# Joining maxima by one reduction, low parts after the transpose, fewer waits: one change to a fused transformer kernel in seven places

## The chip, the core and the metric

One NeuronCore of a Trainium2 chip. The metric is the device time of one execution in microseconds: 2005.45 us, the median of three runs (2004.56 to 2005.53). Engines: PE (TensorE, matrix products, with its weight loads as PEld), DVE (VectorE), ACT (ScalarE), POOL (GpSimd), SP (SyncE, here only a queue of DMAs). Each has a queue of its own, worked off in order; they meet by semaphores only.

## The reference

Two transformer blocks one after the other, everything in float32, on x of 2 x 1024 x 256 and a context of 2 x 77 x 192, 16 heads each:

```
block 0: x += attention(ln(x), ln(x))        16 heads of 64
         x += attention(ln(x), context)      16 heads of 64
         x += (a * gelu(gate)) @ ff_w2       a, gate = split(ln(x) @ ff_w1 + b)
block 1: the same with heads of 16, biases on q, k and v, a causal mask in the
         self attention, gelu(ln(x) @ mlp1) @ mlp2 as the hidden layer
attention: softmax(q k^T / sqrt(d)) v @ w_out + b_out
```

## The kernel before

Stages run one after the other, each in a block that ends in a barrier of all engines: `constants`, `project_norm` (output product, residual sum, layer norm, transposed into `hT`; PE queue: `product(i)`, `turn(i - 1)`), `wide_attention` (self attention of block 0, 34 to 895 us), `cross_attention` wide, `hidden_layer`, `thin_attention`, `cross_attention` thin, `hidden_layer`.

**Wide self attention.** `both(g, b)` works on two heads (group g of 8) of batch b. It has 8 units `u` of two steps; a step is one key tile of 128 for one half `h` of 512 queries (16 steps: half 0, then half 1). In a step PE makes scores for two heads (`scores`: three products of rounded high and low parts, and a fourth that subtracts the row's maximum, from `m_rows`), ACT takes the exponential into one of four buffers `p_buf`, POOL adds them up into `acc` (`both` on POOL, L1235; step 0 and step 8 have no addition), and one unit later PE makes the weighted sums (`weighted`, L998). Between these, PE works ahead for the next batch or group: the `lanes` tables say which item belongs to which unit. Items are `("k", c)` and `("q", c)` (projection; ACT writes the high part, DVE the low part), `("v", c)`, `("m", qt, half)` (one 128 x 512 score tile for each of two heads, only for its maxima: two PE products L935, two DVE reductions L1142 into `mx`), `("t", h)` (L941: the transpose of the maxima of four query tiles, DVE's copy of it into `m_turned` L1150, and from there SP's DMAs into `m_rows` L864) and `("den", h)` (sum over the keys). All items use three PSUM banks in turn, in a fixed order: an item may be filled when DVE (or ACT) has emptied the one three places before. A unit has two `m` items, unit 7 has three, and the first pass (0, 0) has three in some more.

When DVE has reduced the last tile of four (`("m", 3, 1)` in unit 5, `("m", 7, 1)` in unit 1), it joins: `join` (L1157, L1160, L1162) takes the larger of two halves' maxima, its negative rounded, and what the rounding left, each with a wait on the one before. DVE also inverts the denominators (L1171, in quarters; units 2, 3, 6, 7), multiplies the outputs by them (`normalise`, L1177, units 0 and 4 of the next pass) and splits the weights of the next group (`split_w`, L1113, at the end of unit 6, for b = 0).

**Cross attentions.** 32 units n (pair of heads, 512 queries). PE's slot n is `score(n)` (four products L1386), `query(n + 1)` (L1373; in the thin one for every fourth n), `weighted(n - O_LAG)` (L1400), `turn(n - T_LAG)` (L1414), with O_LAG, T_LAG = 2, 1 (wide) and 3, 2 (thin). One PSUM bank `o_ps` holds the weighted sums; DVE's `copy(n - C_LAG)` (L1553 wide, L1556 thin; C_LAG 3 and 4) empties it and raises `o_done`. DVE's slot is `invert(n - 1)`, `copy(n - C_LAG)`, `take(n)` in the wide one and `copy`, `take`, `invert` in the thin one; `take` reads the scores (L1527 or L1519 first), `invert` sums the exponentials (L1541) and inverts (L1545). ACT's slot in the wide one is the copy of the turned probabilities (L1468), the copy of the queries (L1452), the exponential (L1460); thin: exponential, queries, turned. `lin(g, b, per, k)` is the count that a semaphore has after k events of pass (g, b).

## Time and profile before

| | us |
|---|---|
| median of three runs | 2005.45 |
| the profiled execution | 2007.0 |
| its span | 2005.3 |
| busy: PE / PEld / DVE / ACT / POOL | 1788.9 / 1121.9 / 1238.4 / 794.2 / 874.5 |
| L1142 DVE, maxima, x512 | 328.7, mean 0.685 |
| L935 PE, tiles of the maxima, x512 | 130.0, mean 0.502 |
| L1157, L1162 DVE, in the join, x32 each | 30.3 and 34.3, means 0.946 and 1.071 (medians 0.169) |
| L1113 DVE, split of weights, x8 | 0.693 / 2.074 / 2.589 (least, median, most) |
| L1235 POOL, additions, x224 | 532.4, means 2.379 and 2.364 |
| L1386 PE, cross attention scores, x512 | 78.2, mean 0.294 |
| mean granted clock of TensorE | 0.962 |

PE, DVE, ACT and POOL overlap, so their busy times don't add up; what counts in a stage is the engine that never waits and what its idle time waited for. The table's means and medians belong together: where they are far apart, some of the instructions were held. In the rows below, a line in order of time has the start, the duration, the engine, the line, the operation, what it writes and reads, how many were merged, and in brackets the idle time before it with what ended it.

### The profile page before, as it was taken

To read this page: it belongs to the slowest core of one execution; us is meant where nothing else is said; L and a number is where in the kernel's file an instruction comes from. 1 tells how busy PE (TensorE), PEld (TensorE's weight loads), DVE (VectorE), ACT (ScalarE), POOL (GpSimd) and SP (SyncE) were. 2 spreads that over 40 slices of the span, in tenths; PEclk is the share of its full clock that TensorE was granted. 3 is DMA by queue.
4 is the path that set the end of the run, shared out by engine and by line. 5 is a ranking of instruction groups with operands and counts; after the bars stand their busy time and mean duration, and the time that the engine had idled before them with its cause. 6 is when DMAs were issued, how large, how long until landed. Compare 5 with 4: busy or idle time off the path is not lost. (4 is left out here: it accounts for less than half of the span.)

```text
span 2005.3 us, 29769 instructions
## 1 busy us (share of the span) xinstructions
PE 1788.9 (89%) x10124; PEld 1121.9 (56%) x10124; DVE 1238.4 (62%) x2173; ACT 794.2 (40%) x1315; POOL 874.5 (44%) x767
## 2 busy tenths in 40 slices
PE   3789999999999999979899998997798986898799
PEld 2455555555555545538555587886444434565678
DVE  4667777777777777733566443345788853787600
ACT  3234444444444444431344313221366662344340
POOL 1356666666666666661122300021156664366110
PEclk9799999999999999989999898998699998999899
DMA  1000000000000000003000001003244421000101
GB/s 53 6 4 7 4 7 3 6 3 6 3 6 3 6 3 0 1 29 91 24 1 1 1 1 51 21 17 55 51 76 77 87 45 28 8 1 1 29 17 42
DMA packets 49440, 43.69 MB, mean 22 GB/s; under 512 B 17920, under 2 KB 44060, under 8 KB 49343
## 3 DMA queue, kind: packets, MB, share of 16 engines
q1 hardware_dynamic: 44991, 35.86, 8.0%
q0 software_dynamic: 4352, 6.56, 1.6%
q8 instruction: 58, 0.95, 0.2%
q14 instruction: 39, 0.32, 0.0%
HBM read 22.84 MB, written 2.24 MB: 13 GB/s over the span
## 5 line engine op out<-in xcount | busy, mean ns | idle before, releaser
L1235 POOL TENSOR_TENSOR x<-x,sa_p_buf 128x1024 f32<-128x1024 f32 x192 | 456.8, 2379 | 177.6 <-ACT sa_p_buf L1056 169.8
L1056 ACT ACTIVATE sa_p_buf<-sa_score 128x512 f32<-128x512 f32 x512 | 275.9, 597 | 350.8 <-PE sa_score L985 340.7
L1142 DVE TENSOR_REDUCE sa_mx<-sa_front 128x1 f32<-128x512 f32 x512 | 328.7, 685 | 120.4 <-PE sa_front L935 119.0
L998 PE MATMUL sa_out<-sa_p_buf,sa_v_buf 128*64 128x512 f32 x1024 | 246.1, 602 | 0.0
L1722 POOL TENSOR_TENSOR x<-x,bias_out 128x1024 f32<-128x1024 f32 x24 | 55.7, 2348 | 278.6 <-POOLq L1907 152.8
L528 ACT ACTIVATE sa_p_buf<-sa_score 128x1024 f32<-128x1024 f32 (+1 forms) x160 | 141.1, 938 | 86.3 <-PE sa_score L476 86.1
L342 DVE TENSOR_REDUCE sa_mx<-sa_front 128x1 f32<-128x512 f32 (+1 forms) x256 | 155.9, 650 | 26.1 <-PE sa_front L283 23.1
L935 PE MATMUL sa_front<-sa_k_hi,sa_q_hi 64*128 64x512 f32 x512 | 130.0, 502 | 43.3 <-DVE sa_mx L1142 41.2
L935 PEld LDWEIGHTS sa_front<-sa_k_hi,sa_q_hi 64*128 64x128 f32 x512 | 49.6, 186 | 185.1 <-DVE sa_mx L1142 79.4
L1235 POOL TENSOR_TENSOR x<-sa_p_buf 128x1024 f32<-128x1024 f32 x32 | 75.6, 2364 | 133.0 <-ACT sa_p_buf L1056 133.0
L1611 POOL TENSOR_TENSOR ca_probs<-ca_s_sb,ca_inv 128x616 f32<-128x616 f32 x64 | 77.9, 1218 | 125.7 <-DVE ca_inv L1545 125.7
L998 PEld LDWEIGHTS sa_out<-sa_p_buf,sa_v_buf 128*64 128x64 f32 x1024 | 65.0, 136 | 115.3 <-issue 85.8
L1171 DVE RECIPROCAL x<-x 128x128 f32<-128x128 f32 x128 | 111.9, 918 | 26.3 <-ACT x L1069 26.3
L283 PE MATMUL sa_front<-sa_k_top,sa_q_top 59*128 59x128 f32 (+4 forms) x576 | 87.1, 369 | 40.4 <-DVE sa_mx L342 29.5
L283 PEld LDWEIGHTS sa_front<-sa_k_top,sa_q_top 33*128 33x128 f32 (+1 forms) x576 | 53.5, 207 | 102.3 <-DVE sa_mx L342 82.8
L1740 PE MATMUL po_prod<-w_out,o 128*128 128x256 f32 x384 | 92.2, 400 | 20.7 <-PEq L415 11.6
L580 POOL TENSOR_SCALAR_AFFINE_SELECT sa_p_buf<-sa_p_buf 128x128 f32<-128x128 f32 x256 | 65.0, 292 | 96.5 <-ACT sa_p_buf L528 96.4
L981 PE MATMUL sa_score<-sa_q_hi,sa_k_hi 64*128 64x512 f32 x512 | 102.8, 394 | 0.0
L985 PE MATMUL sa_score<-sa_m_rows,sa_one_rows 64*128 64x512 f32 x512 | 102.1, 390 | 0.0
L981 PE MATMUL sa_score<-sa_q_lo,sa_k_hi 64*128 64x512 f32 x512 | 102.1, 391 | 0.0
L981 PE MATMUL sa_score<-sa_q_hi,sa_k_lo 64*128 64x512 f32 x512 | 102.0, 391 | 0.0
L1468 ACT ACTIVATE ca_turned<-ca_t_ps 128x1024 f32<-128x1024 f32 x64 | 65.5, 1023 | 78.2 <-PE ca_t_ps L1414 78.2
(189 smaller groups left out, 3378.4 us busy)
## 6 DMA issues: line engine op xcount, KB each, us to landing
x<-in_x SPq DMA_DIRECT2D x8, 512.0 KB, 8.2
sa_q_stack<-sa_hi SPq DMA_DIRECT2D x64, 64.0 KB, 2.4
sa_k_stack<-sa_hi SPq DMA_DIRECT2D x64, 64.0 KB, 2.4
ff_w<-in_L_xattn_ff_w SPq DMA_DIRECT2D x16, 128.0 KB, 2.1
sa_k_top<-sa_hi POOLq DMA_DIRECT2D x32, 64.0 KB, 2.7
sa_q_top<-sa_hi POOLq DMA_DIRECT2D x32, 64.0 KB, 2.6
sa_q_stack<-sa_lo SPq DMA_DIRECT2D x32, 64.0 KB, 2.4
sa_k_stack<-sa_lo SPq DMA_DIRECT2D x32, 64.0 KB, 2.4
```

The lines of the kernel that those rows point to most:

```text
L283: mm = pe.matmul(bank(i, item, u)[:, c0 + lo_k:c0 + hi_k], q_top[base:base + rows_of, b, r, at], k_top[base:base + rows_of, b, r, k0 + lo_ ...
L342: dve.tensor_reduce(mx[:, b, j, place:place + 1], fr[u][:, 0:n], AX.X, ALU.max).then_inc(drained, 1)
L528: nc.scalar.activation(p_buf[:, n % NPB, 2 * r:2 * r + 2, 0:cols], score_ps[r][:, :, 0:cols], ACT.Exp, scale=SCALE).then_inc(exp_done, 1)
L935: pe.matmul(front_ps[bank(item, j)][:], q_hi[r, b, qt * P:(qt + 1) * P], k_hi[r, b, half * HALF:(half + 1) * HALF], start=True, stop=True) ...
L981: pe.matmul(score_ps[(s * G + j) % NSCORE][:], ks[r, b, keys], qs[r, b, queries], start=(part == 0), stop=False, skip_group_check=True)
L985: pe.matmul(score_ps[(s * G + j) % NSCORE][:], one_rows[r, :], m_rows[r, b, queries], start=False, stop=True, skip_group_check=True).then_ ...
L998: mm = pe.matmul(out_ps[64 * j:64 * j + 64, :], v_buf[:, b, kt, 64 * j:64 * j + 64], p_buf[:, s % NPB, j, :], start=(kt == 0), stop=(kt == ...
L1056: nc.scalar.activation(p_buf[:, s % NPB, j, :], score_ps[n % NSCORE][:], ACT.Exp, scale=SCALE).then_inc(exp_done, 1)
L1142: dve.tensor_reduce(mx[:, b, j, qt, half:half + 1], front_ps[bank(item, j)][:], AX.X, ALU.max).then_inc(drained, 1)
L1171: dve.reciprocal(recip[:, h, at], recip[:, h, at]).then_inc(inverted, 1)
L1235: nc.gpsimd.tensor_tensor(acc[:, h], prev, cur, ALU.add).then_inc(added, 1)
L1740: mm = pe.matmul(prod[i % NPROD][:, t, :], src[:, k, at:at + P], wt[:, k, :], start=(k == 0), stop=(k == KN - 1))
```

## The change

- `join`: one `tensor_reduce` over the two halves' maxima writes `m_row`, with a wait for the last transpose in front; `m_parts` is gone.
- `turn` transposes `m_row` (8 rows in place of 16); DVE's `t` item makes the rounded negative from PSUM, waits, and makes what the rounding left, also from PSUM, into `m_turned[8, 2, 128]`. SP takes it with four DMAs of one row each, not two of two rows.
- `normalise` and `split_w` go from DVE to POOL: the first at steps 0 and 8, which have no addition; the second behind step 13's addition, the very first one ahead of all of POOL's work.
- `wait_free` and the thin attention's `wait_bank` wait once for the two banks of an `m` item; the thin `t` item doesn't wait for its bank; `scores` waits for `q` only in the first pass; the weighted sums of a diagonal bin wait for the mask alone.
- Cross attention: on PE the waits for `q_done` before `query`, `k_set`, `v_set` and most of `s_taken` and `t_done` go. The wait for `o_done` leaves `weighted(n)` and stands before the fourth product of `score(n)`.
- `project_norm`: `turn` doesn't wait for `h_done`.

```diff
 SP, maxima
                     for j in range(G):
-                        r, row = j * 2 * QH, j * dh
-                        sp.dma_start(m_rows[row:row + 2, b, h * HALF:(h + 1) * HALF].bitcast(F32),
-                                     m_turned[r:r + 2 * QH, :].bitcast(F32)).then_inc(max_in, DMA)
+                        for part in range(2):
+                            row = j * dh + part
+                            sp.dma_start(m_rows[row:row + 1, b, h * HALF:(h + 1) * HALF].bitcast(F32),
+                                         m_turned[j * QH:(j + 1) * QH, part, :].bitcast(F32)).then_inc(max_in, DMA)
 PE, maxima and turn
-                    wait_free(g, b, item, 0, ("q", qt // QH), ("k", half))
-                    wait_free(g, b, item, 1)
+                    wait_free(g, b, item, ("q", qt // QH), ("k", half))
...
-                    parts = m_parts[:].bitcast(F32).rearrange("p g s t -> p (g s t)")
-                    pe.transpose(front_ps[bank(item)][0:2 * G * QH, 0:P], parts, ident[:]).then_inc(front_full, 1)
+                    pe.transpose(front_ps[bank(item)][0:G * QH, 0:P], m_row[:].rearrange("p g t -> p (g t)"),
+                                 ident[:]).then_inc(front_full, 1)
 DVE, item t and join
-                        dve.tensor_copy(m_turned[:], fr[0:2 * G * QH, 0:P]).then_inc(drained, 1)
+                        rows = fr[0:G * QH, 0:P]
+                        dve.tensor_scalar(m_turned[:, 0, :], rows, -1.0, None, ALU.mult).then_inc(m_high, 1)
+                        dve.wait_ge(m_high, lin(g, b, HALVES, item[1] + 1))
+                        dve.scalar_tensor_tensor(out=m_turned[:, 1, :], in0=rows, scalar=-1.0,
+                                                 in1=m_turned[:, 0, :].bitcast(F32), op0=ALU.mult,
+                                                 op1=ALU.subtract).then_inc(drained, 1)
...
-                    dve.scalar_tensor_tensor(out=m_row[:], in0=mx[:, b, :, at, 0], scalar=LOWEST, in1=mx[:, b, :, at, 1],
-                                             op0=ALU.max, op1=ALU.max).then_inc(m_step, 1)
-                    dve.wait_ge(m_step, lin(g, b, done, MSTEP * h + 1))
-                    dve.tensor_scalar(m_parts[:, :, 0, :], m_row[:], -1.0, None, ALU.mult).then_inc(m_step, 1)
-                    dve.wait_ge(m_step, lin(g, b, done, MSTEP * h + 2))
-                    dve.scalar_tensor_tensor(out=m_parts[:, :, 1, :], in0=m_row[:], scalar=-1.0,
-                                             in1=m_parts[:, :, 0, :].bitcast(F32), op0=ALU.mult,
-                                             op1=ALU.subtract).then_inc(m_step, 1)
+                    dve.tensor_reduce(m_row[:], mx[:, b, :, h * QH:(h + 1) * QH, :], AX.X, ALU.max).then_inc(joined, 1)
 POOL, before the loop, in it and after it
+                split_w(0)
                 pool.memset(m_rows[:].bitcast(F32), 0.0).then_inc(cleared, 1)
...
                         if kt == 0:
+                            if not is_first(g, b):
+                                normalise(*before(g, b), h)
                             continue
...
                         nc.gpsimd.tensor_tensor(acc[:, h], prev, cur, ALU.add).then_inc(added, 1)
+                        if s == STEPS - 3 and splits(g, b):
+                            split_w(g + 1)
+                    if is_last(g, b):
+                        normalise(g, b, 0)
+                        normalise(g, b, 1)
 cross attention, PE
-                    pe.wait_ge(q_done, n // PQ + 1)
-                    pe.wait_ge(k_set, B * (group(n) + 1))
-                    if n >= 2:
+                    if n % PQ == 0:
+                        pe.wait_ge(q_done, n // PQ + 1)
+                    if n == 0:
+                        pe.wait_ge(k_set, B)
+                    if 2 <= n <= T_LAG:
                         pe.wait_ge(s_taken, n - 1)
                     g, j = group(n), pair(n) * 2 % HR
                     for t in range(TQ):
+                        if t == TQ - 1 and n > O_LAG:
+                            pe.wait_ge(o_done, n - O_LAG)
                         mm = pe.matmul(scores(n)[:, t // 2, 2 * (t % 2):2 * (t % 2) + 2, :],
...
                     pe.wait_ge(t_done, n + 1)
-                    if n >= 1:
+                    if n >= UNITS - O_LAG:
                         pe.wait_ge(o_done, n)
-                    pe.wait_ge(v_set, v_needed(n))
```

## Rows read from the trace of the kernel before

**Rows 1.** Stretches: busy us (instructions) of each engine, clock, DMA; one group of heads.

```profile
173.00:275.20 102.20, 97.55 (x580) 53.12 (x580) 77.07 (x114) 44.63 (x81) 66.47 (x29) 1.00 0.02 5
```

**Rows 2.** Order of time, DVE and PE around a join in unit 5.

```profile
578.72 2.23 DVE L1162 SCALAR_TENSOR_TENSOR sa_m_parts<-sa_m_row,sa_m_parts 128x8 fp32r<-128x8 f32 x1
580.88 2.55 DVE L1142 TENSOR_REDUCE sa_mx<-sa_front 128x1 f32<-128x512 f32 x4
581.61 0.49 PE L935 MATMUL sa_front<-sa_k_hi,sa_q_hi 64*128 64x512 f32 x2 [1.43 <-DVE sa_mx L1142]
...
582.64 0.39 PE L985 MATMUL sa_score<-sa_m_rows,sa_one_rows 64*128 64x512 f32 x2
...
585.57 3.85 DVE L1142 TENSOR_REDUCE sa_mx<-sa_front 128x1 f32<-128x512 f32 x6 [0.34 <-PE sa_front L935]
```

**Rows 3.** Order of time, the split of the weights on DVE.

```profile
635.45 2.06 DVE L1113 SCALAR_TENSOR_TENSOR sa_w_lo<-sa_wqk,sa_w_hi 128x512 fp32r<-128x512 f32 x1
```

**Rows 4.** All instructions of a line: least/median/most ns.

```profile
L1126 DVE TENSOR_TENSOR sa_k_lo<-sa_front,sa_k_hi x32: 682/691/692, 42.6 to 814.4; 128x512 fp32r<-128x512 f32 x32
...
L1541 DVE TENSOR_REDUCE ca_total<-ca_s_sb x64: 782/794/796, 983.2 to 1843.4; 128x8 f32<-128x616 f32 x64
```

**Rows 5.** Order of time, PE: first and last of 20 like stalls.

```profile
173.03 0.49 PE L935 MATMUL sa_front<-sa_k_hi,sa_q_hi 64*128 64x512 f32 x2 [1.48 <-DVE sa_mx L1142]
...
836.69 0.50 PE L935 MATMUL sa_front<-sa_k_hi,sa_q_hi 64*128 64x512 f32 x2 [1.46 <-DVE sa_mx L1142]
```

**Rows 6.** Order of time, PE: stalls of the first pass.

```profile
93.87 0.51 PE L935 MATMUL sa_front<-sa_k_hi,sa_q_hi 64*128 64x512 f32 x2 [0.49 <-DVE sa_k_lo L1126]
...
125.66 0.65 PE L935 MATMUL sa_front<-sa_k_hi,sa_q_hi 64*128 64x512 f32 x2 [2.00 <-DVE sa_mx L1142]
```

**Rows 7.** All instructions of a line, POOL in the cross attentions.

```profile
L1611 POOL TENSOR_TENSOR ca_probs<-ca_s_sb,ca_inv x64: 1216/1217/1221, 984.4 to 1844.5; 128x616 f32<-128x616 f32 x64
```

**Rows 8.** Order of time, the end of the stage.

```profile
888.05 1.98 PE L947 MATMUL sa_front<-x,ones 128*64 128x512 f32 x4 [4.56 <-POOL x L1235]
...
894.11 0.69 DVE L1177 SCALAR_TENSOR_TENSOR o<-o,x 128x512 f32<-128x512 f32 x1
```

**Rows 9.** Order of time, wide cross attention, one slot.

```profile
1002.09 1.88 PE L1373 MATMUL ca_q_ps<-hT,wq 128*128 128x512 f32 x4
...
1004.01 0.60 ACT L1452 ACTIVATE ca_q_sb<-ca_q_ps 128x512 f32<-128x512 f32 x1 [1.75 <-PE ca_q_ps L1373]
...
1005.84 1.22 PE L1386 MATMUL ca_s_ps<-ca_keys,ca_q_sb 128*128 128x154 f32 x8
1006.19 0.64 DVE L1553 COPY o<-ca_o_ps 128x512 f32<-128x512 f32 x1
1006.90 1.88 PE L1373 MATMUL ca_q_ps<-hT,wq 128*128 128x512 f32 x4
...
1007.10 0.80 DVE L1527 TENSOR_REDUCE ca_top<-ca_s_ps 128x8 f32<-128x616 f32 x1 [0.27 <-PE ca_s_ps L1386]
```

**Rows 10.** Order of time, thin cross attention, a period of four slots.

```profile
1737.46 1.88 PE L1373 MATMUL ca_q_ps<-hT,wq 128*128 128x512 f32 x4
...
1744.37 1.22 PE L1386 MATMUL ca_s_ps<-ca_keys,ca_q_sb 128*128 128x154 f32 x8
1745.03 0.69 DVE L1556 COPY o<-ca_o_ps 64x512 f32<-64x512 f32 x1
1745.76 0.80 DVE L1519 TENSOR_TENSOR ca_s_sb<-ca_s_ps,ctx_low 128x616 f32<-128x616 f32 x1
...
1748.24 0.63 DVE L1556 COPY o<-ca_o_ps 64x512 f32<-64x512 f32 x1
...
1751.99 1.88 PE L1373 MATMUL ca_q_ps<-hT,wq 128*128 128x512 f32 x4
```

**Rows 11.** Stretches: the granted clock is the number before the last two.

```profile
1450.00:1460.00 10.00, 8.34 (x77) 4.16 (x81) 8.56 (x19) 6.58 (x8) 3.96 (x16) 1.00 0.08 16
...
120.00:130.00 10.00, 8.00 (x43) 5.02 (x42) 8.99 (x12) 3.88 (x7) 7.35 (x4) 0.83 0.00 1
```

More of the change, by code:

```diff
@@ L237, in sync_early, with wait_bank @@
             load_keys(1)
-    def wait_bank(pe, i, item, k):
-        if PLACE[i, item, k] >= NBANK:
-            pe.wait_ge(drained, PLACE[i, item, k] - NBANK + 1)
+    def wait_bank(pe, i, item):
+        last = PLACE[i, item, width(item) - 1]
+        if last >= NBANK:
+            pe.wait_ge(drained, last - NBANK + 1)
     def bank(i, item, k=0):
@@ L249, in made @@
         g, b = divmod(i, B)
-        wait_bank(pe, i, item, 0)
+        if item[0] != "t":
+            wait_bank(pe, i, item)
         fr = bank(i, item)
@@ L272, in made @@
                 pe.wait_ge(top_in[b], DMA * NTOP * (i // B + 1))
-            wait_bank(pe, i, item, 1)
             c0 = 0
@@ L488, in weighted @@
                             pe.wait_ge(drained, filled(0, ("v", 7)))
-                        pe.wait_ge(exp_done, (unit(i, s) + 1) * PAIRS)
                         if on_diagonal[s]:
                             pe.wait_ge(selected, diagonals(i, s) * PAIRS)
+                        else:
+                            pe.wait_ge(exp_done, (unit(i, s) + 1) * PAIRS)
                         c0 = 0
@@ L888, in _, with wait_free @@
             def _(pe):
-                def wait_free(g, b, item, k, *made_of):
+                def wait_free(g, b, item, *made_of):
                     at = 2 * g + b if isinstance(g, int) else 2 + b
-                    by, value = FREE[at, item, k]
                     counts = [DRAINED[at, part, 0] for part in made_of]
-                    if by == "den":
-                        pe.wait_ge(den_taken, value if isinstance(g, int) else shifted(value, g, HALVES))
-                    elif by == "front":
-                        counts.append(value)
+                    for k in range(2 if item[0] == "m" else 1):
+                        by, value = FREE[at, item, k]
+                        if by == "den":
+                            pe.wait_ge(den_taken, value if isinstance(g, int) else shifted(value, g, HALVES))
+                        elif by == "front":
+                            counts.append(value)
                     if counts:
@@ L954, in front_item @@
                         return
-                    wait_free(g, b, item, 0)
+                    wait_free(g, b, item)
                     if item[0] in ("q", "k"):
@@ L1110, in _ @@
             def _(dve):
-                def split_w(g):
-                    dve.wait_ge(w_high, g + 1)
-                    dve.scalar_tensor_tensor(out=w_lo[:], in0=wqk[:], scalar=1.0, in1=w_hi[:].bitcast(F32), op0=ALU.mult,
-                                             op1=ALU.subtract).then_inc(w_split, 1)
                 def split_h(c):
@@ L1190, in both @@
                             front_item(*of, item)
-                        if u == 0 and not is_first(g, b):
-                            normalise(*before(g, b), 0)
                         if u in (2, 3) and not is_first(g, b):
@@ L1195, in both @@
                             invert(*before(g, b), 1, 2 * u - 3)
-                        if u == 4 and not is_first(g, b):
-                            normalise(*before(g, b), 1)
                         if u in (6, 7):
@@ L1214, in _, with split_w, normalise @@
             def _(pool):
+                def split_w(g):
+                    pool.wait_ge(w_high, g + 1)
+                    nc.gpsimd.tensor_tensor(w_lo[:], wqk[:], w_hi[:].bitcast(F32), ALU.subtract).then_inc(w_split, 1)
+                def normalise(g, b, h):
+                    pool.wait_ge(inverted, lin(g, b, 4 * HALVES, 4 * (h + 1)))
+                    pool.wait_ge(out_taken, lin(g, b, HALVES, h + 1))
+                    dst = out_cols(g, b, h)
+                    nc.gpsimd.tensor_tensor(dst, dst, recip[:, h, :], ALU.mult).then_inc(scaled, 1)
+                split_w(0)
                 pool.memset(m_rows[:].bitcast(F32), 0.0).then_inc(cleared, 1)
@@ L1270, in group @@
         return pair(n) * 2 // HR
-    def v_needed(n):
-        return pair(n) * 2 * dh // VC * B + batch(n) + 1
     with ExitStack() as ctx:
```

41 lines of the change are left out of this document (11 added, 30 removed).

## The prediction

> **What bounds the kernel now.** I read the page first, then a table of stretches, then the order of time in three places. The table by stretch is to show that in the first self attention TensorE is the bound: one group of heads for both batches takes 102.2 us and PE is busy 97.55 of them, DVE 77, POOL 66 [rows 1]. So time there can come only out of PE's idle 4.65 us. The order of time shows where they are: three stalls of 1.42 to 1.43 us a group. Two follow a join of maxima. Its three small DVE instructions should take about 0.17 us each, but the third took 2.23 (and the first nearly as long); the next reduction starts at 580.88 instead of about 579.3, the PSUM bank comes free late, and the second score tile of unit 6 stalls PE for 1.43 us [rows 2]. Two small terms stand there too: PE is released 0.05 us after DVE's first reduction ends (580.88 + 0.68), and its record is 0.49 us long against 0.39 of one that wasn't held, 0.1 for weights loaded in the open. The third follows the split of the weights on DVE, 2.06 us long [rows 3]. What these long instructions have in common is that both inputs, or the one input and the output, lie in SBUF while POOL is inside one of its 2.37 us additions. A DVE instruction with one input in PSUM was never held (L1126: 682 to 692 ns), nor a reduction out of SBUF (L1541: 782 to 796 ns, with POOL busy beside it) [rows 4]. Between 170 and 840 us there are 20 such stalls, each 1.41 to 1.48 us (the first and the last: [rows 5]); 20 x 1.426 = 28.5 us.
>
> **Part by part: first self attention.**
> *Join and turn.* The join becomes one reduction, SBUF to SBUF, a form that was not held; I take 0.17 us. The rounding and the low part are now made behind the transpose, from PSUM, 8 x 128. DVE's t item becomes two instructions and a wait between them, about 0.22 + 0.05 + 0.27 = 0.54 us in place of a copy of some 0.25. With no hold of about 4 us in unit 5, the four reductions of unit 6 start at 579.3 and end at about 581.9, two reciprocals end at 583.65 (they take 1.75), the t pair at about 584.1; PE, now 1.43 us earlier, gives the first tile of unit 7 at 584.1 too (before: 0.34 us of idle DVE there [rows 2]). It is a tie: I take 0.05 us of stall per batch and group, 0.8 in all, and as upper end 0.56 (the second instruction as slow as 0.5 us, and felt in two tiles of unit 7), 8.4 in all. The split moved to POOL removes the third stall for the same reason. Gain 28.5.
> *First pair and small gaps.* The same holds cause 0.49 us before L935 at 93.87 and 2.00 us at 125.66 [rows 6]; with 0.5 for smaller ones between 97 and 119 us I count 3.0. The others up to 120 us come from units with three tiles and stay. Five gaps of 0.15 to 0.25 us at the transpose, which waited for the late parts, add 1.0.
> *Normalisation and split on POOL.* 128x512 elements. POOL did 128x616 in 1.22 us [rows 7] and 128x1024 in 2.38, so 1.0 to 1.2 us each. Per group 4 + 1 of them are 6 us on an engine with 36 us idle, at the step in which it has no addition: hidden in the steady state, and the exponentials' buffers have four steps of slack. Not hidden at the end: in the last pass PE has no tiles of maxima, POOL adds without a pause from 860 to 888 and PE waits 4.56 us for it [rows 8]. One normalisation, that at step 8, falls into this queue: +1.1. The last one, on POOL for 1.2 against DVE's 0.69, is in the open before the block ends [rows 8]: +0.5. At the start the first split ends on POOL about 0.5 us later than by DVE's 0.69, and PE waits for it: +0.5.
> *Four small DMAs for two.* SP issues one in 0.61 us, so the last of a set lands 1.2 us later plus the pair's 0.3. The scores that need them start a unit (7 us) later; nothing, at most +0.5 once at the start. *One wait per pair:* of the two, the later count decides, and it still does; nothing, and at most 0.05 us on 256 pairs, a gain of 12, if a second wait instruction has a price. In cross attention three satisfied waits stand ahead of the scores, and these follow the transposes without a gap [rows 9], so I take nothing.
> Sum of the stage: -28.5 - 3.0 - 1.0 + 0.8 + 1.1 + 0.5 + 0.5 = -29.6 us; bounds -42 and -21.
>
> **Cross attentions.** Waits that others imply go: nothing, for the reason just given. But one is added: the wait for the copy of the output bank now stands before the fourth matmul of the scores; it used to stand before the weighted sums.
> *Wide (first).* PE is busy without a gap, 4.81 us a slot (1002.09 to 1006.90). Scores start 1005.84, queries follow at 1006.90, so the fourth matmul (two records of 0.133 us) streams from 1006.63, its weights load from 1006.53. The copy it will now wait for is the DVE copy of 1006.19, which ends 1006.83 [rows 9]. With the 0.05 and 0.1 us of a release [rows 2] it streams from 1006.98: 0.35 late. The copy doesn't move forward: it stands behind the sum and the reciprocal, these behind the exponential, and ACT reaches that only behind its copy of the queries, which waits for PE (1004.01) [rows 9]. So the loop closes, 4.81 becomes 5.16, in slots 3 to 31: 29 x 0.35 = +10.2.
> *Thin (second).* DVE is the bound in three of four slots. There it copies from 1745.03 to 1745.72 and takes the scores straight after, at 1745.76; PE started them at 1744.37 and they were ready [rows 10]. Now the fourth matmul waits for the copy and the take for the matmul: 0.05 + 0.1 + 0.45 (a fourth matmul's stream to the take, as from 1006.63 to 1007.10 [rows 9]) in place of 0.04. From a take to the end of the next copy DVE needs 3.29, 3.11 (1745.76 to 1748.87) and 3.29 us; with 0.60 behind it the slots are 3.89, 3.71 and 3.89 against 3.33, 3.24 and 3.32, together +1.60. In the slot with the query PE started right at 1751.99, in part under DVE's lateness; now query, sums, turn and scores (4.79) follow a take that is no longer late: +0.15. Four slots: 14.53 (1737.46 to 1751.99) become 16.28; seven groups, the last without its query: +12.1.
> Bounds: 0 for each if the copy were in time, which the rows exclude by 0.3 and 0.65 us; at the other end 0.1 us more in each of the 50 late slots, 5.
> A rule of the Trainium skill bears on the 0.1 (TensorE: Matmul & The Clock Gate, "Step-by-step: what each phase is for"): weight loads are pulled ahead of matmuls in flight when they go to the background buffer. By it the fourth weights could be in place when the wait ends, the cost would be 50 x 0.1 = 5 us less, and the change 12.3 us in place of 7.3. The trace speaks against that: behind a wait that is really late the load started with its matmul.
>
> **Rest.** The second self attention's merged waits, the choice of one wait for diagonal bins and the projections' wait: the remaining wait is the later one in each; 0.
>
> **Sum.** -29.6 + 10.2 + 12.1 = -7.3. The profiled execution took 2007.0 us for a span of 2005.3, so 1999.7; it lies 1.5 over the median of 2005.45. Forecast of the median: 1998.2.
>
> **Rivals.**
> *A. The cross attentions don't pay.* For it: satisfied waits are free [rows 9], and a few tenths of shift in DVE's order would take the copy out of the wide slot. Against: the thin copy ends 0.65 us after the load it would hold, and the order of the queues fixes that. Time 2005.45 - 29.6 = 1975.9. If only one of the two pays, 1986 to 1988.
> *B. DVE's unit 6 stays late.* The t pair at its upper end and the first-pair gains gone: -29.6 + 7.6 + 3 = -19.0, and with 22.3 back +3: 2008.8. Against: 0.34 us of idle DVE at 585.57 [rows 2].
> *C. The clock falls in the cross attentions*, the slower end. TensorE will idle 0.5 to 1 us in each 3.85 us thin slot. The granted clock was 0.83 at 120 to 130 us (part of it at 2.4, part at 1.2 GHz), behind the 2.00 us stall [rows 6, 11]; at half speed a thin slot's 3.0 us of PE work becomes 6, +2.2 on 3.85, so that from four such slots on the change is slower than before; ten make 1998.2 + 22 = 2020. Against: in the second self attention PE is 83% busy at 1450 to 1460 us and the clock is 1.00 [rows 11].
>
> **Chances.** Forecast 0.57 (its own range 1992 to 2004), A with both halves 0.13, one half 0.15, B 0.08, C 0.07. What this kernel's runs can tell from no change is 0.2%, 4 us: under 2001.4 counts as faster, over 2009.5 as slower. Of the forecast's share three quarters lie under 2001.4, and all of A: faster 0.71; same: the rest of the forecast and half of B, 0.18; slower 0.11. The range from 1975 to 2007 takes in nearly all of A and the low half of B.
>
> **What would show it.** No stall over 0.3 us before a score tile of the maxima between 140 and 840 us, and a group at 97.9 to 98.2 in place of 102.1; no DVE instruction of the stage over 1 us; POOL's normalisation 1.0 to 1.2; PE's wait for POOL at the end still there, though starting earlier. Wide cross slots of 5.16 with a gap inside the scores, released by the copy; four thin slots 16.3. I am wrong if the scores stay one block with no gap, if groups stay above 99, or if the clock falls below 1.00 after 1740.

## The result, and the profile after

1980.93 us, the median of four runs (1979.57 to 1986.68), against 2005.49 for the kernel before: ratio 0.9884, interval [0.9863, 0.9904]. The forecast was 1998.2, range 1975 to 2007; so the direction and the range held, and 24.6 us (1.2%, clear of 1 by the interval) were gained where 7.3 were forecast. The time lies outside 1992 to 2004, the range that I gave the forecast itself; the stated range holds it because it was drawn wide enough for rival A. The profiled execution took 1982.1 us, its span is 1980.3.

The first matmul of PE in each stage, in both traces, shows where. The last two columns are what the stage itself gained or lost, and what my sum had for it (the -38.0 and the -29.6 include the later start of the first row):

| first matmul of | before | after | offset | stage | forecast |
|---|---|---|---|---|---|
| wide self attention (L917) | 38.96 | 39.60 | +0.64 | | +0.5 |
| its output product (L1731) | 899.15 | 861.18 | -37.97 | -38.0 | -29.6 |
| wide cross attention, queries | 964.70 | 925.89 | -38.81 | -0.8 | 0 |
| its output product | 1138.07 | 1109.95 | -28.12 | +10.7 | +10.2 |
| hidden layer's output product | 1300.16 | 1271.08 | -29.08 | -1.0 | 0 |
| thin self attention's output product | 1675.67 | 1639.76 | -35.91 | -6.8 | 0 |
| thin cross attention, queries | 1722.77 | 1686.40 | -36.37 | -0.5 | 0 |
| its output product | 1851.26 | 1827.01 | -24.25 | +12.1 | +12.1 |
| end of the span | 2005.3 | 1980.3 | -25.0 | -0.8 | 0 |

The two self attentions gained more than I had for them, the cross attentions cost what I had. The four entries of -0.5 to -1.0 are 3.1 us that no term of mine has. Two of them, 1.8 us, are from the clock and not from an edit: experiment 2 below has the code of before in these stretches and takes 64.74 and 161.13 us there (before 65.55 and 162.09, after 64.71 and 161.13), at the changed kernel's granted clock (0.97 and 0.96, for 0.96 and 0.95 before). For the other two, 1.3 us, no run tells the cause apart.

**Wide self attention.** One group of heads for both batches, as in [rows 1] (us, then busy us with the count of instructions for PE, PEld, DVE, ACT and POOL, granted clock, DMA share, GB/s):

```profile
173.17:269.99 96.82, 96.63 (x584) 52.69 (x582) 65.10 (x105) 44.63 (x81) 72.72 (x34) 1.00 0.02 6
```

It was 102.20 us with 4.65 idle; now 96.82 with 0.2. So the group lost 5.4 us, not the 4.0 to 4.3 that I expected. Around the join in unit 5, in order of time (start, duration), the answer to [rows 2]:

```profile
549.72 2.56 DVE L1138 TENSOR_REDUCE sa_mx<-sa_front 128x1 f32<-128x512 f32 x4 [1.60 <-PE sa_front L936]
552.32 0.17 DVE L1158 TENSOR_REDUCE sa_m_row<-sa_mx 128x8 f32<-128x16 f32 x1
...
555.08 1.29 DVE L1138 TENSOR_REDUCE sa_mx<-sa_front 128x1 f32<-128x512 f32 x2 [2.59 <-PE sa_front L936]
```

```profile
554.54 0.50 PE L936 MATMUL sa_front<-sa_k_hi,sa_q_hi 64*128 64x512 f32 x2
...
555.82 0.50 PE L936 MATMUL sa_front<-sa_k_hi,sa_q_hi 64*128 64x512 f32 x2
```

DVE is idle for 2.59 us behind the join instead of being late, and the second item of unit 6 begins 1.28 us after the first and isn't held; before, 2.86 us lay between them. The join and the split, all instances (least/median/most ns; the split is the answer to [rows 3]):

```profile
L1158 DVE TENSOR_REDUCE sa_m_row<-sa_mx x32: 169/170/172, 63.9 to 815.0; 128x8 f32<-128x16 f32 x32
```

```profile
L1195 POOL TENSOR_TENSOR sa_w_lo<-sa_wqk,sa_w_hi x8: 1267/1272/1283, 38.3 to 707.3; 128x512 fp32r<-128x512 f32 x8
```

At the stage's end PE waits longer for POOL (5.12 for 4.56, [rows 8]), and POOL's last normalisation takes 1.26 us where DVE's took 0.69:

```profile
849.56 1.98 PE L948 MATMUL sa_front<-x,ones 128*64 128x512 f32 x4 [5.12 <-POOL x L1226]
...
855.67 1.26 POOL L1201 TENSOR_TENSOR o<-o,x 128x512 f32<-128x512 f32 x1 [5.03 <-DVE x L1165]
```

**Cross attentions.** In the wide one the slot is 5.16 us long, from one query product to the next, as forecast; it was 4.81 [rows 9]. The scores take 1.58 us in place of 1.22, because the load for the fourth product waits for the copy:

```profile
960.88 1.88 PE L1363 MATMUL ca_q_ps<-hT,wq 128*128 128x512 f32 x4
...
964.63 1.58 PE L1380 MATMUL ca_s_ps<-ca_keys,ca_q_sb 128*128 128x154 f32 x8
964.98 0.64 DVE L1544 COPY o<-ca_o_ps 128x512 f32<-128x512 f32 x1
965.67 0.30 PEld L1380 LDWEIGHTS ca_s_ps<-ca_keys,ca_q_sb 128*128 128x128 f32 x2 [0.33 <-DVE o L1544]
```

In the thin one the fourth product stands behind the copy of `o_ps` too. In each period three of four slots are held, by 0.46, 0.41 and 0.59 us; the period is 16.35 us (16.28 forecast) and was 14.53 [rows 10]. The copy, the weight load and the two records of the product, and below them the durations of the five score records around this place:

```profile
1724.53 0.69 DVE L1547 COPY o<-ca_o_ps 64x512 f32<-64x512 f32 x1
1725.28 0.30 PEld L1380 LDWEIGHTS ca_s_ps<-ca_keys,ca_q_sb 128*128 128x128 f32 x2 [0.69 <-DVE o L1547]
1725.28 0.53 PE L1380 MATMUL ca_s_ps<-ca_keys,ca_q_sb 128*128 128x154 f32 x2 [0.46 <-DVE o L1547]
```

```profile
L1380 PE MATMUL ca_s_ps<-ca_keys,ca_q_sb x5: 292/293/399, 1724.3 to 1725.5; 128*128 128x154 f32 x5
```

The held weights are loaded 0.05 us after the copy's end, with their product, and its record is 0.40 us long where the others are 0.29. So the 0.1 us of a load in the open stays in the price. I had weighed a rule of the Trainium skill (TensorE: Matmul & The Clock Gate, "Step-by-step: what each phase is for"), by which weight loads are pulled ahead of matmuls in flight; in this trace the load wasn't pulled ahead past the wait.

**Thin self attention.** Here is a gain that I hadn't seen. In front of the passes the items `m` are bound by DVE. Before:

```profile
1388.97 0.80 PE L283 MATMUL sa_front<-sa_k_top,sa_q_top 33*128 33x512 f32 x2 [0.84 <-DVE sa_mx L342]
1390.61 0.80 PE L283 MATMUL sa_front<-sa_k_top,sa_q_top 33*128 33x512 f32 x2 [0.84 <-DVE sa_mx L342]
```

After:

```profile
1359.49 0.80 PE L284 MATMUL sa_front<-sa_k_top,sa_q_top 33*128 33x512 f32 x2 [0.78 <-DVE sa_mx L343]
1361.06 0.80 PE L284 MATMUL sa_front<-sa_k_top,sa_q_top 33*128 33x512 f32 x2 [0.78 <-DVE sa_mx L343]
```

1.64 us from one to the next became 1.575, though DVE's reductions are the same. In the steady passes one pass takes 30.0 us instead of 30.6. The stage's 6.8 us fall into four parts, by its transpositions: 1.4 up to the first one, 3.0 from the first to the second, 4.1 from there to the eighth, and 1.7 lost behind it. The 3.0 are not mainly from the edits. The stretch from the first to the second transposition in the kernel before, in the changed one, and in experiment 2, which has the old waits there:

```profile
1415.19:1454.62 39.43, 33.40 (x197) 18.02 (x198) 26.83 (x50) 16.77 (x21) 8.69 (x27) 0.69 0.37 65
```

```profile
1384.67:1421.07 36.40, 31.00 (x198) 16.48 (x198) 26.65 (x50) 16.70 (x21) 8.65 (x27) 0.74 0.39 70
```

```profile
1374.97:1411.49 36.52, 30.49 (x197) 16.44 (x198) 26.76 (x50) 16.70 (x21) 8.68 (x27) 0.76 0.40 69
```

The granted clock is the number before the last two. With the old waits and a clock of 0.76 the stretch is nearly as short as in the changed kernel (0.74); the kernel before had 0.69.

### The profile page after: what moved, and what is told of

The parts are those of the page before. It is cut to its first block and busy times, and to the rows that moved or that the text cites. A ratio compares the mean times of both kernels' runs of the same rounds, so it can differ in the third digit from the quotient of the medians.

```text
span 1980.3 us, 29088 instructions
## 1 busy us (share of the span) xinstructions
PE 1790.0 (90%) x10124; PEld 1113.7 (56%) x10124; DVE 1143.8 (58%) x2101; ACT 794.7 (40%) x1315; POOL 923.1 (47%) x807
## 5 line engine op out<-in xcount | busy, mean ns | idle before, releaser
L936 PE MATMUL sa_front<-sa_k_hi,sa_q_hi 64*128 64x512 f32 x512 | 129.6, 502 | 10.7 <-DVE sa_mx L1138 9.3
L1731 PE MATMUL po_prod<-w_out,o 128*128 128x256 f32 x384 | 90.5, 395 | 21.4 <-PEq L416 11.7
L1380 PE MATMUL ca_s_ps<-ca_keys,ca_q_sb 128*128 128x154 f32 x512 | 91.7, 304 | 13.6 <-DVE o L1547 10.2
```

The costliest lines, as they stand in the source:

```text
L936: pe.matmul(front_ps[bank(item, j)][:], q_hi[r, b, qt * P:(qt + 1) * P], k_hi[r, b, half * HALF:(half + 1) * HALF], start=True, stop=True) ...
L1731: mm = pe.matmul(prod[i % NPROD][:, t, :], src[:, k, at:at + P], wt[:, k, :], start=(k == 0), stop=(k == KN - 1))
```

## The experiments

Two theories. Mine: DVE's instructions with all operands in SBUF, reductions apart, are held by POOL's additions, which makes the stalls of the wide self attention; the `o_done` wait alone costs the 22 us; and a second wait instruction in front of a held PE item has a price, which is the thin self attention's gain. The rival: the waits that were merged or removed explain the wide gain too, and the long DVE instructions are DVE's own.

The experiments ran on four chips, each beside runs of the kernel before. The runs of the kernel before lie 5 to 12.5 us apart on one chip (2002.3 to 2015.3 in all), and they go with the granted clock, from 0.964 in the fastest to 0.958 in the slowest. So a ratio is always to the kernel before on the same chip, and a few us between two medians decide nothing; what decides are the lengths of stages in the traces. Where the clock differed in them, it is said.

**1. The wait for `o_done` back**

```diff
-                        if t == TQ - 1 and n > O_LAG:
-                            pe.wait_ge(o_done, n - O_LAG)
...
-                    if n >= UNITS - O_LAG:
+                    if n >= 1:
                         pe.wait_ge(o_done, n)
```

> The changed kernel with one edit taken back: in both cross attentions the wait for `o_done` stands again before `weighted(n)` and is gone from the fourth product of `score(n)`. Theory: this wait alone made both cross attentions longer. From the changed kernel's trace to this one the wide one then loses 10.7 us (the offset of PE's output product against the kernel before went from -38.8 us at its start to -28.1 at its end) and the thin one 11.6 (from -35.8 to -24.2), so 1980.9 - 22.3 = 1958.6 us, and a period of four slots of the thin one is 14.53 us again and not 16.35. Rival: the slots are longer because other waits left PE's queue (q_done, k_set, v_set, t_done, s_taken) and the engines now meet in another order; then the time stays near 1981 us, above 1975 in any case.

Measured: 1961.77 us (1958.96 to 1964.15), ratio to before 0.9759 [0.9733, 0.9785]. The wide cross attention (first queries to output product) takes 173.7 us, against 184.1 in the changed kernel and 173.4 before; the thin one 130.5 against 140.6 and 128.5. The period is 14.58 us:

```profile
1707.59 1.88 PE L1363 MATMUL ca_q_ps<-hT,wq 128*128 128x512 f32 x4
1722.17 1.88 PE L1363 MATMUL ca_q_ps<-hT,wq 128*128 128x512 f32 x4
```

So the one wait is the whole loss: 10.4 and 10.1 us, some 20 of the 22 expected (in the thin stage's first 25 us the clock was 0.86 here and 0.93 in the changed kernel). The other waits that left PE's queue gave nothing in these stages.

**2. Only the wide self attention changed**

The function `wide_attention` of the changed kernel in the kernel before; no other line.

> The kernel before, with only the wide self attention of the changed one (the join by one reduction, low parts from PSUM, normalise and split on POOL, one wait per pair there). Theory: that stage gives 38.0 us at the first output product behind it and all the rest of the kernel keeps its length, the thin self attention too, so 2005.5 - 38.0 = 1967.5 us. Rival for the thin self attention's 6.8 us: it follows from the state in which the earlier stages leave the chip (clock, queues) and not from its own edits; then it is 6.8 us shorter here too and the time is near 1960.7 us.

Measured: 1973.2 us (1966.26 to 1974.48), 37.9 under the kernel before on this chip (2011.06), ratio 0.9823 [0.9799, 0.9846]; the profiled run is the 1966.3. The stage's output product begins at 860.43 (-38.7), the wide cross attention takes 173.6, and from the hidden layer's output product to that of the thin self attention it is 375.1 us as before (375.5), not 368.7. The items are 1.64 us apart again. My theory holds in the main. Up to its first transposition the thin self attention takes 115.0 us again (113.6 in the changed kernel), and 180.4 from the second to the eighth (176.3): 5.6 us are from its own edits. Of the 3.0 us between the first and the second, 2.9 are here too, without these edits.

**3. and 4. One wait or two, and in which order**

```diff
 3
-        last = PLACE[i, item, width(item) - 1]
-        if last >= NBANK:
-            pe.wait_ge(drained, last - NBANK + 1)
+        for k in range(width(item)):
+            if PLACE[i, item, k] >= NBANK:
+                pe.wait_ge(drained, PLACE[i, item, k] - NBANK + 1)
 4
         last = PLACE[i, item, width(item) - 1]
+        if width(item) == 2 and last >= 3 * NBANK:
+            pe.wait_ge(drained, last - 3 * NBANK + 1)
```

> The changed kernel with `wait_bank` of the thin self attention once per bank again, two waits ahead of the two products of an item `m` (the waits that left the diagonal bins and the item `t` stay out). Theory: the second wait instruction has a price when the first one was really late, 0.065 us for each item that DVE holds and about 0.1 in the passes; it explains the 6.8 us that the stage lost, so 1980.9 + 6.8 = 1987.7 us, and the items `m` in front of the passes are 1.64 us apart again and not 1.575. Rival: the gain is from the waits that left the diagonal bins (exp_done) and the item `t`; then the time stays at 1981 us and the items are 1.575 us apart.

> The changed kernel; in the thin self attention a wait that was met long ago (for the bank three rounds back) is put in front of the one wait of each item `m`, so that there are two wait instructions again, the late one last. Two theories of why two waits cost more: (a) each wait instruction that stands between the held one and the first product costs, the order matters: here the extra one comes before the late one and is done while PE is held anyway, so 0, 1981 us and 1.575 us between the items; (b) the extra instruction costs wherever it stands, since it is one more instruction of PE's queue for each item; then +6 to +7 us, 1987 to 1988 us and 1.64 us between the items.

Measured: 1987.95 us (1987.93 to 1995.43), ratio 0.9894 [0.9870, 0.9917], and 1992.9 us (1986.86 to 1995.95), ratio 0.9915 [0.9883, 0.9947]. Both intervals overlap that of the changed kernel, so the medians can't show 6.8 us; the traces can. The same items in both, held by 0.84 to 0.85 again and 1.64 us apart:

```profile
1357.89 0.79 PE L284 MATMUL sa_front<-sa_k_top,sa_q_top 33*128 33x512 f32 x2 [0.84 <-DVE sa_mx L343]
1359.53 0.80 PE L284 MATMUL sa_front<-sa_k_top,sa_q_top 33*128 33x512 f32 x2 [0.85 <-DVE sa_mx L343]
```

```profile
1357.32 0.79 PE L286 MATMUL sa_front<-sa_k_top,sa_q_top 33*128 33x512 f32 x2 [0.84 <-DVE sa_mx L345]
1358.96 0.79 PE L286 MATMUL sa_front<-sa_k_top,sa_q_top 33*128 33x512 f32 x2 [0.84 <-DVE sa_mx L345]
```

From the second to the eighth transposition the stage takes 180.3 and 180.4 us; it took 180.4 before and 176.3 in the changed kernel. Up to the first transposition it is 114.9 in both (115.0 and 113.6). So the merged wait is the gain, and the waits that left the diagonal bins and the item `t` gave nothing there. Of the two explanations in 4, (a) fell: a wait that was met long ago and stands ahead of the late one costs the same 0.065 us as one behind it. It is the second wait instruction as such that costs, for an item that is held; why isn't shown by these runs.

The median of 4 and the profiled run of 3 lie 6.0 and 7.5 us above their fastest. The trace of 3 shows why: 25 us at the start of the thin self attention, at half the clock (1.2 GHz), where the changed kernel had 0.85 in the same stretch.

```profile
1394.08:1419.08 25.00, 24.29 (x116) 13.32 (x114) 12.72 (x23) 11.00 (x15) 5.99 (x20) 0.51 0.38 61
```

```profile
1396.08:1421.08 25.00, 23.89 (x165) 11.99 (x163) 18.23 (x36) 14.76 (x19) 8.12 (x25) 0.85 0.43 72
```

First to second transposition: 43.4 us in 3, 36.4 in the changed kernel. The kernels are alike there but for the waits, and experiment 2, with the old waits, takes 36.5. The scatter of the other runs goes with the clock too: of the runs of 3, those of 1987.9 us have a mean granted clock of 0.963 to 0.964 and the one of 1995.43 has 0.959; in 4 it goes from 0.964 (1986.86) to 0.958 (1995.95). In which stretch they lost it isn't known, since only one run of each has a trace.

**5. The old join**

`join`, the copy of the turned rows, the transposition and the DMAs as before; split and normalisation stay on POOL.

> The changed kernel with the join of the kernel before: three small DVE instructions in a row on SBUF, 16 rows transposed, one copy on DVE, two DMAs. The split of the weights and the normalisation stay on POOL, the waits stay merged. Theory: the join is worth its 13 stalls in unit 5 at 1.58 us each (the held item begins 2.86 us after its partner and not 1.28), 0.30 us for each of 15 transpositions in unit 1 and 1.5 us in the first pass, so + 26.5 us: 1980.9 + 26.5 = 2007.4 us, and L1162's mean is above 1 us again. Rival: the stalls of 1.43 us came from DVE's total load in the unit (the join and the normalisation together) and not from the long instructions; without the normalisation on DVE the old join costs less than half of that, under 1994 us.

Measured: 2009.77 us (ten runs, 2008.73 to 2014.21), ratio to before 1.0004 [0.9986, 1.0022]; the output product at 888.00, + 26.8 against the changed kernel. 14 stalls of PE of 1.4 to 1.6 us. All instances of the third instruction, which reads and writes 8 elements a partition:

```profile
L1160 DVE SCALAR_TENSOR_TENSOR sa_m_parts<-sa_m_row,sa_m_parts x32: 166/1194/2269, 63.8 to 841.6; 128x8 fp32r<-128x8 f32 x32
```

The join is worth 27 of the stage's 38 us, as expected. DVE's load isn't the cause: the normalisation had left it. Without the join's gain the whole change would have given nothing.

**6. and 11. The split on DVE, at two places**

```diff
+                def split_w(g):        # on DVE, as before; on POOL it goes
...
 6, DVE's loop, behind the items q, k, v, t
+                        if u == UNITS - 2 and splits(g, b):
+                            split_w(g + 1)
 11, in place of that, behind unit 7's inversions
+                        if u == UNITS - 1 and splits(g, b):
+                            split_w(g + 1)
 both: split_w(0) on DVE too, ahead of the stage; none on POOL
```

> The changed kernel with the split of the weights on DVE again, at the end of unit 6 (and ahead of the stage). Theory: DVE's instruction, both inputs in SBUF, is held while POOL adds and takes 2.1 to 2.6 us in place of 0.69 (in the first pass 0.69); 7 stalls of PE of 1.58 us come back = 11.1, the start gets 0.6 shorter: 1980.9 + 10.5 = 1991.4 us. Rival: with the join shortened DVE is early enough in unit 6 and hides the split: at most + 2 us, under 1983 us.

Measured: 1988.19 us (1985.69 to 1989.53), ratio 0.9887 [0.9852, 0.9923]; the output product at 864.18, + 3.0. Neither theory had that: the instruction takes 0.67 us and PE is held by 0.33 us behind it, 0.47 us for each of seven groups. The two engines around it:

```profile
317.96 0.67 DVE L1114 SCALAR_TENSOR_TENSOR sa_w_lo<-sa_wqk,sa_w_hi 128x512 fp32r<-128x512 f32 x1
```

```profile
315.52 10.23 POOL L1229 TENSOR_TENSOR x<-x,sa_p_buf 128x1024 f32<-128x1024 f32 x4 [0.53 <-ACT sa_p_buf L1057]
```

Two additions take 4.84 us, so the first ends at about 317.94, and DVE's begins there. The four take 10.23 and not 9.7. The second alone:

```profile
317.96 2.92 POOL L1229 TENSOR_TENSOR x<-x,sa_p_buf 128x1024 f32<-128x1024 f32 x1
```

It takes 2.92 us in place of 2.37. DVE came first, by less than 0.01 us, and POOL waited.

> The run before with the split of the weights on DVE (1988.2 us) showed it at 0.67 us in all seven passes, at + 0.47 us each and not 1.58: it began at the moment at which one addition of POOL ended, and POOL's four additions took 10.23 us and not 4 x 2.42, so POOL waited. Here the same instruction stands in unit 7 behind the inversions, some 0.5 us into an addition of POOL (POOL's fourth one runs from about 712.9 to 715.1 there). Theory: which of the two is held is a matter of who comes first. The split is held until the addition ends, 2.0 to 2.4 us long, DVE's copy of `v` comes that much later, it had about 0.4 us to spare, PE loses 1.6 to 2.0 us in each of seven passes: the last item `v` 11 to 14 us later than in the changed kernel (804.75), 1992 to 1996 us. Rival: the split of 2.06 us in the kernel before had another cause; the instruction takes 0.67 us here too, and costs 0.3 us each, the last `v` at 807 us, 1985 us.

Measured: 1993.51 us (1992.64 to 1997.91), ratio 0.9921 [0.9905, 0.9938].

```profile
L1114 DVE SCALAR_TENSOR_TENSOR sa_w_lo<-sa_wqk,sa_w_hi x8: 691/2282/2406, 38.4 to 717.3; 128x512 fp32r<-128x512 f32 x8
```

```profile
709.35 9.71 POOL L1229 TENSOR_TENSOR x<-x,sa_p_buf 128x1024 f32<-128x1024 f32 x4 [0.53 <-ACT sa_p_buf L1057]
719.02 1.72 POOL L1205 TENSOR_TENSOR o<-o,x 128x512 f32 x1
```

Held in all seven passes, until 719.6: POOL's fourth addition ends at 719.06, and DVE's own 0.6 us follow, for which POOL's normalisation then waits (1.72 us for 1.29). So who comes first decides.

The Trainium skill has this rule (SBUF — State Buffer, "Who interferes with whom"): a DVE instruction with two inputs in SBUF contends with a GpSimd instruction that reads SBUF, and the order of issue decides which of the two is blocked. 6 and 11 agree: in 6 POOL's addition takes 2.92 us, in 11 DVE's split 2.28.

The price in 11 was smaller than forecast, 8.0 us at the last item `v` (812.75) and not 11 to 14: of the 2.28 us PE lost 1.2, so DVE had about 1.1 to spare there and not 0.4. The same instruction costs 0.47 or 1.2 us, by its place alone; in the kernel before 1.58.

**7. Two waits in the wide self attention**

```diff
                     for k in range(2 if item[0] == "m" else 1):
+                        if k and counts:
+                            pe.wait_ge(drained, ...)      # the first bank's and the operands'
+                            counts = []
                         by, value = FREE[at, item, k]
```

> The changed kernel with two wait instructions again in front of each item `m` of the wide self attention. Theory: nothing holds PE there any more in the steady passes, an additional wait that is already met costs nothing: 0 in the passes, and 0.063 us for each of the some ten items that DVE holds ahead of the first pass, in all + 0.5 to 1 us: 1981.5 us. Rival: what the wide stage gave beyond the forecast 29.6 us (8.4 us: 0.15 us more for each of 20 stalls, 0.30 in each unit 1) is the price of the second wait instruction, as in the thin self attention; then + 7 to 8 us, 1988.5 us.

Measured: 1981.74 us (1979.83 to 1986.25), ratio 0.9860 [0.9823, 0.9898]; the last item `v` at 804.93 (+ 0.2), the output product + 0.4. The rival is out: the waits gave nothing where PE isn't held.

**8. and 12. A better version**

The wait of 1, and at the end of the wide self attention:

```diff
 POOL, step 8 of the last pass has no normalisation; behind the loop
+                        normalise(*before(g, b), 1)
                         normalise(g, b, 0)
-                        normalise(g, b, 1)
 DVE, behind the last inversions
+                        last_normalise(g, b)
 12 also: split_w(0) on DVE behind split_h(0)
```

> The changed kernel with `o_done` back before `weighted(n)` in both cross attentions (worth 22 us, as measured) and two edits at the end of the wide self attention: in the last pass POOL does the normalisation of the pass before only after its last addition, and the last normalisation of all is DVE's. Theory: the chain that ends the stage is POOL's additions, the sums on PE, the inversion; the first edit takes 1.27 us out of it, the second exchanges 1.26 us of POOL for 0.69 of DVE: 1.8 us less than 1959.0 = 1957.2 us. PE's wait before the last sums is 3.9 and not 5.1 us. Rival: the sums wait for ACT's last exponentials and not for POOL's order of work, then the first edit gives nothing, 1958.4 us and the wait stays at 5.1.

> The best version so far (`o_done` back before `weighted(n)`, POOL's normalisation out of the last pass's chain, the last one on DVE), and the very first split of the weights on DVE again, behind its first part of `h_lo`; the seven later ones stay on POOL. Theory: the first projection then begins as in the kernel before, 0.5 to 0.6 us earlier (POOL's split takes 1.27 us, DVE's 0.69), and nothing else changes: 1960.5 - 0.55 = 1959.9 us in the median. Rival: DVE is what the first items wait for, its 0.69 us come back at the first item `m`, and the first `v` begins at 68.5 us as in the changed kernel; 1960.5 us.

Measured: 1960.46 us (1957.44 to 1964.64), ratio to before 0.9752 [0.9714, 0.9789], and 1961.38 (1957.40 to 1964.12), 0.9756 [0.9740, 0.9773]. In 8:

```profile
845.80 1.98 PE L948 MATMUL sa_front<-x,ones 128*64 128x512 f32 x4 [3.93 <-POOL x L1234]
...
851.87 0.69 DVE L1116 SCALAR_TENSOR_TENSOR o<-o,x 128x512 f32<-128x512 f32 x1
```

The wait is 3.93 as expected. In 12 the output product begins 1.8 us earlier than in 1 (859.29 for 861.11): 1.27 from the wait, 0.3 from the start (the first `v` begins 0.54 earlier, 67.97 for 68.51, and 0.3 of it is left at the last one), 0.2 from the last normalisation. In 8 it is 4.1 us, but 2.4 of these are from the clock between 60 and 75 us. In the medians neither can be told from 1. With 1 these are the fastest versions: in the spans of the profiled runs they are 18 to 21 us below the changed kernel (1980.3 us against 1962.3, 1959.6 and 1962.0).

**9. Short additions on POOL**

```diff
-                        nc.gpsimd.tensor_tensor(acc[:, h], prev, cur, ALU.add).then_inc(added, 1)
+                        nc.gpsimd.tensor_tensor(acc[:, h, :, 0:32], prev[:, :, 0:32], cur[:, :, 0:32], ALU.add).then_inc(added, 1)
```

> The kernel before, whose additions of the exponentials on POOL in the wide self attention are done for 32 of 512 queries per head only (the sums of the others, and so their denominators, are left out; all else is as before). No DVE instruction is changed. Theory: DVE's instructions with both operands in SBUF are held by POOL's instruction that runs at the time; with short ones the join's third instruction is 0.17 us long in the mean and not 1.07, the split 0.69 us, the 20 stalls of 1.43 us are gone, the last item `v` begins 36 to 39 us earlier, and PE's last wait for POOL (4.56 us) shrinks to 1 or less: 2005.5 - 38 - 4 = 1963.5 us. Rival: the long instructions are DVE's own latency in a chain of dependent instructions; then they stay above 1 us in the mean and only the wait at the end shrinks: 2001.5 us.

This is the kernel before, and it leaves out the sums of 480 of 512 queries for each head. Measured: 1966.04 us (1963.98 to 1973.12), ratio 0.9791 [0.9766, 0.9815]. No DVE instruction was changed, and yet:

```profile
L1162 DVE SCALAR_TENSOR_TENSOR sa_m_parts<-sa_m_row,sa_m_parts x32: 166/168/169, 64.1 to 819.2; 128x8 fp32r<-128x8 f32 x32
```

```profile
L1113 DVE SCALAR_TENSOR_TENSOR sa_w_lo<-sa_wqk,sa_w_hi x8: 661/664/693, 38.4 to 707.4; 128x512 fp32r<-128x512 f32 x8
```

No stall above 0.4 us is left between 115 and 850 us, the last `v` begins at 808.5 (-34.9, where I had expected 36 to 39), the output product 40.3 us earlier. This shows the cause, with no edit on DVE or PE.

**10. The normalisation on DVE**

```diff
 DVE's loop, units 0 and 4; of the last two one ahead of the last inversions, one behind them; none on POOL
+                        if u == 0 and not is_first(g, b):
+                            normalise(*before(g, b), 0)
```

> The changed kernel with the normalisation of the outputs on DVE again (units 0 and 4, the last ones at the end). Its STT has both inputs in SBUF, as the split has. Theory: it comes at steps 0 and 8, in which POOL has no addition (the step before may still run into it), and in these units DVE has time to spare, so that PE sees nothing in the passes; at the end POOL's two normalisations leave the chain: 0 in the passes and - 1.2 to - 1.8 us at the end, 1979.4 us. Rival: it is held as the split was, DVE is late in units 0 and 4 and PE loses up to 1.58 us in each of 30 places: up to + 47 us; any stall of PE above 1 us between 115 and 849 us would show it.

Measured: 1980.65 us (1977.14 to 1983.24), ratio 0.9861 [0.9836, 0.9886]. No stall, the last `v` at 804.39 (-0.4), the output product at 859.98 (-1.2). Moving it to POOL was worth nothing in the passes and cost 0.8 us at the end, in place of the 1.6 (1.1 + 0.5) of my sum.

## Why the prediction was right, and where its sizes were off

**Right.** What was late in the wide self attention and why (5, 9); that nothing new becomes late there; that the third kind of stall goes with the split; the start + 0.64 for + 0.5; both cross attentions, to 0.5 us (1): a wait moved from a product that stands behind other work to one that comes earlier in PE's queue, in front of DVE's copy. Against 1, at nearly the same clock, the wide one cost 10.4 us for the 10.2 of my sum. That a second wait which is met costs nothing is right where PE isn't held (7).

**Right by luck.** I took the 0.1 us of a load in the open from 0.49 us for a held record of the tiles of maxima against 0.39 for one that wasn't held. These are two different products. A tile's record is 0.50 us long when nothing holds it, as the rows around unit 6 above show, so this comparison shows nothing of a load. The held scores, 0.40 for 0.29, gave the same size.

**The term 20 x 1.426.** The number in brackets is the gap from the modelled end of one record to the next start. But the record of the product ahead overlaps its follower by 0.16 us when nothing is held; a stall costs the difference of the distances, 2.86 - 1.28 = 1.58. This is (1.58 - 1.426) x 20 = 3.1 us.

**What I left out.** In unit 1 the transposition waited for the three-instruction join. I listed only the five gaps of 0.15 us and more, 1.0 us in all; the others are 0.14 long, and each of the 15 passes lost 0.30 us there (6.88 us from one item to the next became 6.58), 4.5 us in all. So 3.5 were missing.

**Terms that didn't come.** The tie in unit 7, for which I had taken 0.8 us, cost nothing. From the last `v` to the output product the changed kernel takes 0.6 us more (56.4 for 55.8), where I had 1.6. With 3.1 and 3.5 these are the 8.4 us that the stage gave beyond the forecast. POOL's normalisation takes 1.26 to 1.31 us, not 1.0 to 1.2; it is hidden in the passes.

**The term 0 for merged waits.** In the thin self attention PE is held by DVE at nearly each item `m` in front of the passes and at five or six in each pass, which my sum treated like the wide one. Its bound of 0.05 us an instruction had nearly the size (measured: 0.065, and 0.12 for each held item of the passes), but I took zero from rows where the wait was met. It is 5.5 us in the two stretches that experiments 2, 3 and 4 bear out, and at most about 6.4, the difference of the whole stage to experiment 2 (375.1 for 368.7). The rest of the 6.8 us is the clock's.

**The clock.** My sum has no term for it. The profiled runs compare a mean granted clock of 0.962 with one of 0.965, and the stretches that experiment 2 has without the edits show that part of the 25.0 us is from this: 1.8 us in two small entries and most of the 3.0 us between two transpositions, less what was lost behind the eighth.

**The split.** I priced it like the other stalls, and for the kernel before that is right (1.58 a group); but it wasn't a property of the instruction. With the join short, DVE meets POOL at another moment, and the split on DVE would have cost 0.47 (6). So the seven stalls were partly the join's as well.

**The rivals.** A (cross attentions don't pay) came near in time, 1975.9, nearer than the forecast, and was wrong in its reason: both cross attentions got longer, by what I had. B didn't occur (no stall in unit 6), nor C (the granted clock is 1.00 from 1711 to 1811 us, in the middle of the thin cross attention). My sign "below 1.00 after 1740" was too wide: it is 0.66 from 1865 to 1875 us, behind the cross attention, and was 0.53 from 1890 to 1900 in the kernel before.

## What to carry to other kernels

An 8-element instruction can take 2 us: look at the spread of a line's durations (166/1194/2269), not its mean, and at what another engine was doing. Before a wait is moved earlier in a queue "because it is met anyway", take the time at which its event happens in each slot and compare it with the new place. And price a wait instruction where the engine is held, not where it is free.

## What the runs showed of the hardware that I had not expected

The holding between DVE and POOL goes both ways: DVE's instruction that begins between two additions runs in 0.67 us and POOL's next one takes 2.92 us for 2.37 (6); one that begins inside waits until the addition's end and ends 0.55 us behind it (11).

A second wait instruction on PE costs 0.065 us an item when the item is held, even if the added wait was met long ago and stands first (1.64 us between items for 1.575, in 3 and in 4); where nothing is held it costs nothing that can be seen (+ 0.2 us over the whole wide stage, in 7).

At the start of the thin self attention the clock came back from 1.2 to 2.4 GHz at different moments in runs of nearly the same program (0.51 in 3, 0.70 in the kernel before and 0.85 in the changed one, over like 25 us). From the first to the second transposition this is 43.4 us in 3 against 36.5 in 2, which both have the old two waits: 7 us.
